# Gate and up projections of six blocks as seven block products instead of eight, with the order of work planned anew

## The chip, the cores and the metric

The kernel runs on one core of one Trainium2 chip. The number compared is the time of one execution on the device in microseconds (us), median of several runs. Engines: TensorE (PE; PEld is its weight load), VectorE (DVE), ScalarE (ACT), GpSimd (POOL), SyncE (SP, which here only starts DMAs).

## What is computed

The input x has 2 sequences of 4096 tokens with 256 features. Three branches are added:

```python
xn = layernorm(x)
h = tanh(xn @ W1.T + b1); s = h @ w2.T + b2          # a score per token
e = exp(s - max(s)); ctx = cumsum(e * xn) / cumsum(e)  # running mean over the sequence
attn = tanh(concat(ctx, xn) @ Wc.T + bc)
gate = xn @ (w_gate / 127).T; up = xn @ (w_up / 127).T   # integer weights, 768 hidden units
ffn = (silu(gate) * up) @ (w_down / 127).T
out = x + attn + ffn
```

The change touches `gate` and `up`.

## The kernel before, in words

The 8192 tokens are 16 blocks of 512. All of a block's matmuls are float16 with operands split into a high and a low part: x (times 1024) is `xt16[:, s, k, tokens]`, s = 0 high, s = 1 low, k one of the two halves of the 256 features. Integer weights are exact in float16 and need one part. For each block i the work is made of named steps:

- `Lp` or `Ln`, `Xh`, `Xm`, `Tx`: normalise, high part, low part, transposing DMAs into `xt16`.
- `Ss`, `S`, `Th`, `Sv`: scores (bias put into the bank by ACT, 12 matmuls of 256 columns, tanh, weighted sum). After the last block of a sequence the small softmax steps `V0`, `M1`, `Ex`, `M2` and so on.
- `Gg` and `Gu` (function `hidden`, matmul at L809): gate and up of hidden tile j (0 to 5, 128 units each), each 4 matmuls of 512 columns (two k, two parts of x) into one PSUM bank.
- `Sg` (ACT, L970): silu of the gate's bank to SBUF. `H` (DVE, L1204): times up, written back into up's bank. `Hh` (ACT, L977): high part of that to SBUF. `Hl` (DVE, L1209): low part.
- `D` (L777), two steps of 24 matmuls of 256 columns; its sum is added to x by `Da` (DVE, L1213).
- `N` (POOL, L1316 and L1321), `Sc` (DVE scan, L1227), `Ch` (ACT, L991), `Cl` (POOL, L1349): running mean. `Cs` (ACT, L915), `C` (L829 and L777, two steps of 24 matmuls of 256 columns), `Ct` (ACT, L984), `Ca` (DVE, L1218): the attention output. `Er`, `Ro`, `O` are DMAs.

The order on every engine is fixed when the program is built. `due_times` gives every step a due time, `STEP` a cost, and the class `Plan` hands out steps by due time as soon as it takes their needs (`needs`) to be met; it also chooses which of the 8 PSUM banks a group of matmuls gets, and so on whom it waits. Each engine then runs its list strictly in order, with semaphores between engines. `SEED_AHEAD` says how early ACT may put a bias into a bank; `SLACK` is time the plan leaves between a step and its user on another engine (TensorE 1.0 us, ACT and DVE 0.3 us).

## Time and profile before

| | us |
|---|---|
| median of 3 runs | 393.57 |
| the three runs | 391.73, 393.60, 393.57 |
| span of the profiled execution (first to last instruction) | 390.1 |
| PE busy | 384.7 |
| DVE, ACT, POOL busy | 290.2, 234.3, 213.2 |

The page gives the profiled execution by its span; its time on the clock of the runs isn't recorded, so what lies around the span is between 1.6 and 3.5 us, by the lowest and the highest run. In 40 slices of the span PE's busy digit is 9 in all but the first and the last; the granted clock is at its full level throughout.

### The profile page before, as it was taken

How to read it: one execution, taken by the hardware profiler on the slowest of the kernel's cores; microseconds unless marked ns; L12 is line 12 of the kernel's file. 1: busy time of each engine (PE TensorE's matmuls, PEld its weight loads, DVE VectorE, ACT ScalarE, POOL GpSimd, SP SyncE). 2: the span in 40 equal slices, each digit the busy share in tenths (PEclk: the TensorE clock that was granted, in tenths of full speed). 3: DMA queues.
4: the chain of work that ended last, by engine and by line, in shares of the span. 5: the costliest groups of instructions: out<-in, count | busy, mean ns of one | idle time of the engine just before them, and what ended most of it. 6: DMA issues, size and time to landing. Idle time of an engine off the chain costs nothing.

```text
span 390.1 us, 7869 instructions
## 1 busy us (share of the span) xinstructions
PE 384.7 (99%) x2735; PEld 268.3 (69%) x2735; DVE 290.2 (74%) x604; ACT 234.3 (60%) x436; POOL 213.2 (55%) x301
## 2 busy tenths in 40 slices
PE   8999999999999999999999999999999999999996
PEld 4557586666666686766877777768677676776765
DVE  6799999879697896966679965876776766754351
ACT  4785667498975659786466575463563644536260
POOL 1658797775529999895244415765455654502000
PEclk9999999999999999999999999999999999999999
DMA  8965356556644233676300014042131340100001
GB/s 257 332 220 86 84 106 175 93 150 92 170 96 98 54 99 66 134 145 101 81 29 29 28 41 154 27 150 79 43 94 46 80 106 4 54 29 28 29 27 62
DMA packets 55776, 36.82 MB, mean 94 GB/s; under 512 B 31922, under 2 KB 51635, under 8 KB 55731
## 3 DMA queue, kind: packets, MB, share of 16 engines
q1 hardware_dynamic: 55440, 35.99, 36.8%
q8 instruction: 24, 0.39, 0.4%
q10 hardware_dynamic: 290, 0.26, 0.2%
q14 instruction: 22, 0.17, 0.2%
HBM read 20.45 MB, written 8.45 MB: 74 GB/s over the span
## 4 chain that ended last, share of the span: by engine, by line
PE 99%; DVE 0%; issue 0%
PE bank L777 44%; PE bank L809 42%; PE bank L829 9%; PE bank L1474 1%; PE bank L756 1%; PE bank L748 0%; PE bank L741 0%; PE bank L1481 0%; DVE sg L1501 0%; PE bank L884 0%; PE bank L890 0%; DVE xres L1213 0%; PE bank L883 0%; PE bank L877 0%; PE bank L872 0%
## 5 line engine op out<-in xcount | busy, mean ns | idle before, releaser
L809 PE MATMUL bank<-xt,narrow 128*128 128x512 f16 x768 | 177.6, 379 | 0.0
L809 PEld LDWEIGHTS bank<-xt,narrow 128*128 128x128 f16 x768 | 75.2, 98 | 75.0
L777 PE MATMUL bank<-narrow,wide 128*128 128x256 f16 x792 | 96.4, 273 | 0.0
L777 PE MATMUL bank<-narrow,xt 128*128 128x256 f16 x744 | 90.2, 273 | 0.0
L1349 POOL TENSOR_TENSOR wide<-ex,wide 128x512 f16<-128x512 f32 x32 | 40.3, 1277 | 86.9 <-ACT wide L991 86.9
L970 ACT ACTIVATE sg<-bank 128x512 f32<-128x512 f32 x96 | 56.9, 595 | 49.9 <-PE bank L809 47.6
L777 PEld LDWEIGHTS bank<-narrow,xt 128*128 128x128 f16 x744 | 72.8, 98 | 18.0
L1204 DVE SCALAR_TENSOR_TENSOR bank<-bank,sg 128x512 f32<-128x512 f32 x96 | 66.1, 693 | 24.5 <-PE bank L809 22.2
L777 PEld LDWEIGHTS bank<-narrow,wide 128*128 128x128 f16 x792 | 77.5, 98 | 9.4
L977 ACT ACTIVATE wide<-bank 128x512 f16<-128x512 f32 x90 | 53.2, 594 | 46.8 <-DVE bank L1204 42.5
L1209 DVE TENSOR_TENSOR wide<-bank,wide 128x512 f16<-128x512 f32 x90 | 60.3, 677 | 9.7 <-ACT wide L977 8.5
L1227 DVE TENSOR_TENSOR_SCAN ex<-rows,ex 128x512 f32<-128x512 f32 x32 | 56.0, 1749 | 1.6 <-POOL ex L1321 1.6
L1321 POOL TENSOR_TENSOR ex<-ex,rows 128x512 f32<-128x512 f32 x32 | 43.6, 1364 | 8.9 <-DMA rows<-scratch 6.5
L1316 POOL TENSOR_TENSOR ex<-xt 128x512 f32<-128x512 f16 x32 | 46.4, 1449 | 0.2
L1213 DVE TENSOR_TENSOR xres<-bank,xres 128x512 f32<-128x512 f32 (+1 forms) x33 | 22.0, 667 | 29.9 <-PE bank L777 29.8
L829 PE MATMUL bank<-narrow,wide 128*128 128x256 f16 x312 | 38.3, 273 | 0.0
L984 ACT ACTIVATE bank<-bank 128x512 f32<-128x512 f32 (+1 forms) x33 | 18.8, 570 | 30.7 <-PE bank L777 30.7
L915 ACT ACTIVATE bank<-every 128x512 f32<-128x512 f32 (+1 forms) x63 | 37.1, 595 | 0.2 <-issue 0.2
L829 PEld LDWEIGHTS bank<-narrow,wide 128*128 128x128 f16 x312 | 30.5, 98 | 7.0
L1218 DVE TENSOR_TENSOR xres<-bank,xres 128x512 f32<-128x512 f32 x28 | 19.3, 688 | 17.8 <-ACT bank L984 17.7
L1189 DVE CUSTOM_DVE_ANT_0 bank<-bank,every 128x256 f32<-128x256 f32 x64 | 25.5, 443 | 4.8 <-ACT bank L964 4.8
L964 ACT ACTIVATE bank<-bank 128x512 f32<-128x512 f32 x32 | 18.7, 585 | 7.4 <-PE bank L777 7.4
(109 smaller groups left out, 259.0 us busy)
## 6 DMA issues: line engine op xcount, KB each, us to landing
rows<-scratch SPq DMA_DIRECT2D x16, 512.0 KB, 5.3
out_y<-xres SPq DMA_DIRECT2D x31, 256.0 KB, 2.1
xres<-in_x SPq DMA_DIRECT2D x15, 512.0 KB, 5.0
xt<-xt SPq DMA_TRANSPOSE x56, 2.5
wide<-in_wg SPq DMA_DIRECT2D x2, 384.0 KB, 5.3
wide<-in_wu SPq DMA_DIRECT2D x2, 384.0 KB, 6.6
wide<-in_wd SPq DMA_DIRECT2D x1, 768.0 KB, 8.7
wide<-in_wc SPq DMA_DIRECT2D x1, 512.0 KB, 10.4
```

Of the source, the lines that this page charges most:

```text
L777: return pe.matmul(dst, lhs, rhs, start=False, stop=stop, skip_group_check=True)
L809: mm = pe.matmul(b[:, :], pg.up(which, k, j), pg.xn(sx, k, tok), start=n == 0, stop=n == len(todo) - 1)
L829: mm = pe.matmul(dst, lhs, rhs, start=n == 0, stop=n == len(todo) - 1)
L915: act.activation(b[:, 0:n * D].rearrange("p (t d) -> p t d", t=n), row.to_broadcast([P, n, D]), ACT.Copy, scale=pg.sum_up).then_inc(done, 1)
L970: act.activation(sg[:, m % SG_RING, :], bank_of(pg, "Gg", i, n)[:, :], ACT.Silu, scale=pg.silu_scale).then_inc(a_sg, 1)
L977: act.activation(pg.h(0, m, slice(0, BLK)), bank_of(pg, "Gu", i, n)[:, :], ACT.Copy).then_inc(a_h, 1)
L1204: dve.scalar_tensor_tensor(out=dst, in0=b[:, :], scalar=pg.up_scale, in1=sg[:, m % SG_RING, :], op0=ALU.mult, op1=ALU.mult).then_inc(v_h, 1)
L1209: dve.tensor_tensor(pg.h(1, m, slice(0, BLK)), bank_of(pg, "Gu", i, n)[:, :], pg.h(0, m, slice(0, BLK)), ALU.subtract).then_inc(v_hlo, 1)
L1227: dve.tensor_tensor_scan(t, rows[:, i % 2, 1, :], t, 0.0 if first else ex[:, (i - 1) % EX_RING, n, BLK - 1:BLK], ALU.mult, ALU.add).then_i ...
L1316: pool.tensor_tensor(dst, xt16[:, 0, k, tok], xt16[:, 1, k, tok], ALU.add).then_inc(g_x, 1)
L1321: pool.tensor_tensor(dst, src, rows[:, i % 2, 0, :], ALU.mult).then_inc(g_ex, 1)
L1349: pool.tensor_tensor(pg.ctx(1, i, k, slice(0, BLK)), ex[:, i % EX_RING, k, :], pg.ctx(0, i, k, slice(0, BLK)), ALU.subtract).then_inc(g_cl ...
```

## The change

For blocks 9 to 14 (`FAST`) the steps `Gg` and `Gu` are gone. A pair of hidden tiles (a group q, 0 to 2) is computed with tokens in two halves A and B of 256, features in two halves k = 0, 1, and gate and up together: that is a 2 x 2 by 2 x 2 product of blocks, usually 8 block products, here 7 (`Qa` to `Qg`), each 4 matmuls of 256 columns (two hidden tiles, two parts of x). It needs four sums of weights (`Ks`, `sums16`, once) and, for each of these blocks, four sums of x (`Nt` on ACT normalises once more, `Tf` on POOL forms the sums, `Uh` on ACT and `Um` on POOL split them, `Ux` on SP transposes them by DMA into `forms`).

The seven products share partial sums. `Zs` (ACT) copies Qa's bank to a second one; `Qd` goes onto the first (gate of A), `Qc` onto the second; `Zv` (ACT) copies that to SBUF; `Qe` goes on top; `Yv` (ACT) copies Qb's bank to SBUF; `Wa` (DVE) adds it to Qe's bank into SBUF (up of B); `Qf` then goes onto that bank (up of A); `Qg` goes onto Qb's bank and `Ya` (DVE) adds Zv's copy (gate of B). `H` and `Hh` follow as before, but the product H is written to SBUF (`up_of`); the low part of the second of each pair moves from DVE to POOL (`Hp`). Storage comes from regions of `xres` and `xt` whose blocks are done, so `O` of blocks 0 to 4 gets semaphores of its own (`s_home`).

Besides, `SEED_AHEAD` goes from 2.5 to 9.05, the due times of `C` and `D` are tables, and `CHAIN` = 0.3 takes the place of TensorE's slack of 1.0 for the new steps: the whole order is planned anew.

```diff
-SEED_AHEAD = 2.5
+SEED_AHEAD = 9.05
+CHAIN = 0.3
+    "Qa": (TE, 0.44, 0.68), "Qb": (TE, 0.44, 0.68), "Qc": (TE, 0.44, 0.68), ...
+    "Wa": (VE, 0.62, 0.75), "Ya": (VE, 0.62, 0.75), "Ks": (VE, 3.8, 3.9), "Hp": (PO, 1.3, 1.4),
+FAST = tuple(range(9, 15))
+GROUPS = KH // 2
-        ctx = 38.0 + 3.7 * i if i < LAST else NBLK * KH
-        place += [(ctx + pr, ("C", i, pr)) for pr in shares(i)]
+        place += [(C_AT[i] + C_STEP * pr, ("C", i, pr)) for pr in shares(i)]
...
+            def product(kind, i, q):
+                first, second = slice(0, PAIR), slice(PAIR, BLK)
+                gate = ("Gg", i, 2 * q + (kind in ("Qb", "Qg")))
+                b = bank_of(pg, *gate) if kind in ("Qa", "Qb", "Qd", "Qg") else bank_of(pg, "Gu", i, 2 * q)
...
+                elif kind == "Qc":
+                    pe.wait_ge(a_zs, pg.nth("Zs", i, q))
...
+                    w, of_x, done = sums16[:, 1, :], lambda s: forms(i)[:, s, 1, second], p_qc
+                elif kind == "Qd":
+                    pe.wait_ge(a_zs, pg.nth("Zs", i, q))
+                elif kind == "Qe":
+                    pe.wait_ge(a_zv, pg.nth("Zv", i, q))
+                elif kind == "Qf":
+                    pe.wait_ge(v_wa, pg.nth("Wa", i, q))
+                else:
+                    pe.wait_ge(a_yv, pg.nth("Yv", i, q))
...
+                opens = kind in ("Qa", "Qb")
+                for e in range(2):
+                    j = 2 * q + e
+                    for s in range(2):
+                        mm = pe.matmul(b[:, e * PAIR:(e + 1) * PAIR], w[:, j * P:(j + 1) * P], of_x(s),
+                                       start=opens and (e, s) == (0, 0), stop=s == 1, skip_group_check=True)
+                mm.then_inc(done, 1)
...
+            elif kind == "Zs":
+                b = open_bank(act, pg, "Gu", i, 2 * n)
+                act.wait_ge(p_qa, pg.nth("Qa", i, n))
+                act.activation(b[:, :], bank_of(pg, "Gg", i, 2 * n)[:, :], ACT.Copy).then_inc(a_zs, 1)
+            elif kind == "Zv":
...
+                act.wait_ge(p_qc, pg.nth("Qc", i, n))
+                act.activation(later[group_number(i, n) % 2], bank_of(pg, "Gu", i, 2 * n)[:, :], ACT.Copy).then_inc(a_zv, 1)
...
+            elif kind == "Wa":
+                back, at = before_group(i, n, 2), group_number(i, n) % 2
+                if back:
+                    dve.wait_ge(g_hlo, pg.nth("Hp", back[0], 2 * back[1] + 1))
...
+                dve.wait_ge(a_yv, pg.nth("Yv", i, n))
+                dve.wait_ge(p_qe, pg.nth("Qe", i, n))
+                dve.tensor_tensor(second_up[at], half(bank_of(pg, "Gu", i, 2 * n)[:, :]), half(first_sum),
+                                  ALU.add).then_inc(v_wa, 1)
+            elif kind == "Ya":
+                b = bank_of(pg, "Gg", i, 2 * n + 1)
+                dve.wait_ge(a_zv, pg.nth("Zv", i, n))
+                dve.wait_ge(p_qg, pg.nth("Qg", i, n))
+                dve.tensor_tensor(b[:, :], b[:, :], later[group_number(i, n) % 2], ALU.add).then_inc(v_ya, 1)
...
+            elif kind == "Tf":
+                pool.wait_ge(a_nt, pg.nth("Nt", i, 1))
+                before = FORM_STEPS * (pg.nth("Tf", i, 0) - 1)
+                (a0, a1), (b0, b1) = ([xnat[:, pr, :, k * P:(k + 1) * P] for k in range(KD)] for pr in range(2))
+                pool.tensor_tensor(a0, b0, a0, ALU.subtract).then_inc(g_tf, 1)
...
+            elif kind == "Um":
+                pool.wait_ge(a_uh, pg.nth("Uh", i, k))
+                pool.tensor_tensor(xt16[:, k, :, D:BLK], xnat[:, k, :, :], xt16[:, k, :, 0:D],
+                                   ALU.subtract).then_inc(g_um, 1)
+            elif kind == "Hp":
+                m = KH * i + k
+                pool.wait_ge(a_h, pg.nth("Hh", i, k))
+                pool.tensor_tensor(half(pg.h(1, m, slice(0, BLK))), up_of(i, k),
+                                   half(pg.h(0, m, slice(0, BLK))), ALU.subtract).then_inc(g_hlo, 1)
```

What stands on TensorE around `D` of block 10. In the order of before L809 with `x4` is one `Gg` or `Gu`, L829 and L777 from `narrow,wide` are a `D` or the second half of a `C`, L777 from `narrow,xt` the first half of a `C`:

```order
L777 MATMUL bank5<-narrow,xt 128x256 x12
L777 MATMUL bank5<-narrow,wide 128x256 x12
L829 MATMUL bank6<-narrow,wide 128x256 x12
L777 MATMUL bank6<-narrow,wide 128x256 x12
L809 MATMUL bank7<-xt,narrow 128x512 x4
L829 MATMUL bank4<-narrow,wide 128x256 x12
L777 MATMUL bank4<-narrow,wide 128x256 x12
L809 MATMUL bank1<-xt,narrow 128x512 x4
L777 MATMUL bank2<-narrow,xt 128x256 x12
```

In the order of after, L1007 is one of the seven products: from `xt,narrow` it is Qa or Qd, from `xt,xres` Qg, from `xres,narrow` Qf, from `xres` alone Qb, Qc or Qe. L1031 and L933 are what L829 and L777 were:

```order
L1007 MATMUL bank4<-xres 128x256 x4
L1007 MATMUL bank7<-xres,narrow 128x256 x4
L1031 MATMUL bank5<-narrow,wide 128x256 x12
L933 MATMUL bank5<-narrow,wide 128x256 x12
L1007 MATMUL bank6<-xt,narrow 128x256 x4
L1031 MATMUL bank0<-narrow,wide 128x256 x12
L933 MATMUL bank0<-narrow,wide 128x256 x12
L1007 MATMUL bank4<-xres 128x256 x4
L1007 MATMUL bank3<-xt,xres 128x256 x4
L1007 MATMUL bank2<-xt,narrow 128x256 x4
L1007 MATMUL bank5<-xres 128x256 x4
L933 MATMUL bank1<-narrow,xt 128x256 x12
L933 MATMUL bank1<-narrow,wide 128x256 x12
```

`D` and `C` stand near where they stood, but the products between them wait for one another through other engines. The first row is Qc of block 11's second group, into bank4. After Qf of the group before, `D`, Qd and `D` comes Qe into the same bank4, which waits for `Zv`; after Qg, Qa, Qb and half of `C` comes Qf into bank4, which waits for `Wa`.

What stands on VectorE at the same place, before. L1204 is `H`, L1209 `Hl`, L1218 `Ca`, L1227 `Sc`, L1213 `Da`:

```order
L1209 TENSOR_TENSOR wide<-bank3,wide 128x512
L1209 TENSOR_TENSOR wide<-bank0,wide 128x512
L1218 TENSOR_TENSOR xres<-bank5,xres 128x512
L1227 SCALAR_TENSOR_TENSOR ex<-rows,ex 128x512
L1213 TENSOR_TENSOR xres<-bank6,xres 128x512
L1213 TENSOR_TENSOR xres<-bank4,xres 128x512
L1204 SCALAR_TENSOR_TENSOR bank1<-bank1,sg 128x512
L1209 TENSOR_TENSOR wide<-bank1,wide 128x512
```

And after. L1459 is `H` (written to `xt`; from `xt,sg` for the second of a pair), L1490 `Hl`, L1499 `Ca`, L1508 `Sc`, L1494 `Da`, L1469 `Wa`, L1475 `Ya`:

```order
L1459 SCALAR_TENSOR_TENSOR xt<-bank7,sg 128x2x256
L1499 TENSOR_TENSOR xres<-bank2,xres 128x512
L1459 SCALAR_TENSOR_TENSOR xt<-xt,sg 128x2x256
L1494 TENSOR_TENSOR xres<-bank5,xres 128x512
L1490 TENSOR_TENSOR wide<-xt,wide 128x512
L1508 SCALAR_TENSOR_TENSOR ex<-rows,ex 128x512
L1494 TENSOR_TENSOR xres<-bank0,xres 128x512
L1469 TENSOR_TENSOR xt<-bank4,xres 128x2x256
L1475 TENSOR_TENSOR bank3<-bank3,xres 128x512
L1459 SCALAR_TENSOR_TENSOR xt<-bank4,sg 128x2x256
L1459 SCALAR_TENSOR_TENSOR xt<-xt,sg 128x2x256
```

`Wa`, for which TensorE's next Qf waits, stands behind `H`, `Da`, `Hl`, `Sc` and `Da` in VectorE's list. `H` of the second of a pair and `Hl` now read two operands from SBUF, where before one of them came from PSUM.

## Rows read from the trace of the kernel before

**Rows 1.** The page: busy time by engine, then PE and its clock in 40 slices

```profile
PE 384.7 (99%) x2735; PEld 268.3 (69%) x2735; DVE 290.2 (74%) x604; ACT 234.3 (60%) x436; POOL 213.2 (55%) x301
...
PE   8999999999999999999999999999999999999996
...
PEclk9999999999999999999999999999999999999999
```

**Rows 2.** The page: the chain that ended last, by engine

```profile
PE 99%; DVE 0%; issue 0%
```

**Rows 3.** Waits of PE, whole span: engine line waited for: us, times, longest

```profile
PE bank L1474 <- DVE sg L1501: 1.6, 1, 1.6
```

**Rows 4.** The chain in order of time: start us, us, what

```profile
276.76 5.18 PE bank L809 x24
...
375.78 10.49 PE bank L777 x96
```

**Rows 5.** Groups of instructions: line engine op names shapes count | busy us, mean ns | idle before

```profile
L777 PEld LDWEIGHTS bank<-narrow,wide 128*128 128x128 f16 x792 | 77.5, 98 | 9.4
```

**Rows 6.** Busy time in the stretch of blocks 9 to 14: window, length, then each engine

```profile
213.35:354.90 141.55, 141.55 (x1019) 99.55 (x1018) 98.84 (x141) 73.62 (x133) 68.93 (x54) 1.00 0.22 66
```

**Rows 7.** Groups of DVE in that stretch: the scan

```profile
L1227 DVE TENSOR_TENSOR_SCAN ex<-rows,ex 128x512 f32<-128x512 f32 x19 | 30.9, 1628 | 0.0
```

**Rows 8.** Single lines: duration ns min/median/max, first and last start

```profile
L1227 DVE TENSOR_TENSOR_SCAN ex<-rows,ex x32: 1267/1756/2318, 122.6 to 341.4; 128x512 f32<-128x512 f32 x32
...
L1209 DVE TENSOR_TENSOR wide<-bank,wide x90: 656/680/693, 31.5 to 377.3; 128x512 f16<-128x512 f32 x90
...
L1349 POOL TENSOR_TENSOR wide<-ex,wide x32: 1148/1157/2084, 126.6 to 354.8; 128x512 f16<-128x512 f32 x32
...
L1316 POOL TENSOR_TENSOR ex<-xt x32: 1138/1155/2084, 118.3 to 337.6; 128x512 f32<-128x512 f16 x32
...
L1321 POOL TENSOR_TENSOR ex<-ex,rows x32: 1262/1270/2081, 119.5 to 339.7; 128x512 f32<-128x512 f32 x32
```

**Rows 9.** Timeline near 136 us, DVE and then POOL: start us, us, instruction

```profile
136.29 2.18 DVE L1227 TENSOR_TENSOR_SCAN ex<-rows,ex 128x512 f32<-128x512 f32 x1
138.40 0.66 DVE L1209 TENSOR_TENSOR wide<-bank,wide 128x512 f16<-128x512 f32 x1
138.98 0.67 DVE L1213 TENSOR_TENSOR xres<-bank,xres 128x512 f32<-128x512 f32 x1
...
136.24 1.16 POOL L1349 TENSOR_TENSOR wide<-ex,wide 128x512 f16<-128x512 f32 x1
137.35 2.07 POOL L1316 TENSOR_TENSOR ex<-xt 128x512 f32<-128x512 f16 x1
```

**Rows 10.** Timeline, 359 to 362 us: from one engine to the next

```profile
359.39 0.70 DVE L1204 SCALAR_TENSOR_TENSOR bank<-bank,sg 128x512 f32<-128x512 f32 x1 [2.23 <-PE bank L809]
360.19 0.60 ACT L977 ACTIVATE wide<-bank 128x512 f16<-128x512 f32 x1 [1.07 <-DVE bank L1204]
...
361.74 1.89 PE L809 MATMUL bank<-xt,narrow 128*128 128x512 f16 x8
361.94 0.58 ACT L984 ACTIVATE bank<-bank 128x512 f32<-128x512 f32 x1 [1.16 <-PE bank L777]
```

**Rows 11.** Timeline of ACT near 87 us: three instructions that wait for nobody

```profile
86.54 0.60 ACT L970 ACTIVATE sg<-bank 128x512 f32<-128x512 f32 x1
87.02 0.62 ACT L915 ACTIVATE bank<-every 128x512 f32<-128x512 f32 x1
87.54 0.64 ACT L947 ACTIVATE xt<-xt 128x512 f16<-128x512 f32 x1
```

**Rows 12.** Groups: VectorE on float16 with both inputs in SBUF

```profile
L1261 DVE TENSOR_TENSOR xt<-xt 128x768 f16<-128x768 f16 x1 | 1.5, 1504 | 0.0
...
L1258 DVE TENSOR_TENSOR xt<-xt 128x768 f16<-128x768 f16 x1 | 0.9, 918 | 0.0
```

More of the change, by code:

```diff
@@ L87 @@
 POOLED = tuple(range(1, 9))
+FAST = tuple(range(9, 15))
+GROUPS = KH // 2
+LOW_POOL = (1,)
+HOME = tuple(range(5))
 FIRST_T = 2
@@ L177, in due_times @@
         due[st] = now
-        now += STEP[st[0]][1]
+        now += STEP[st[0]][1] if st[0] not in ("Gg", "Gu") or st[1] not in FAST else 0.0
         end[st] = now
@@ L341, in needs @@
     if kind == "D":
-        return [(("Hl", i, k), 0.2 * k) for k in range(KH)] + ([(("Ct", i, x), 0)] if seeded(i, x) else []) \
+        low = [((low_of(half_of(x)), i, 2 * q + half_of(x)), 0.4 * q) for q in range(GROUPS)] if seven else \
+            [(("Hl", i, k), 0.2 * k) for k in range(KH)]
+        return low + ([(("Ct", i, x), 0)] if seeded(i, x) else []) \
             + [(("D", i, x - 1) if x else ("Wdh", 0, 0), 0)]
@@ L486, in start @@
         group = closed_by(st)
+        if st[1] in FAST and not self.wide and st[0] in ("H", "Hl"):
+            group = ("Gu", *st[1:]) if st[0] == "H" and st[2] % 2 == 0 else None
         if group is not None:
@@ L1193, in vector_step @@
                 m = KH * i + n
-                b = bank_of(pg, "Gu", i, n)
+                second = pg.fast(i) and n % 2
+                b = None if second else bank_of(pg, "Gu", i, n)
                 if pg.wide:
```

268 lines of the change are left out of this document (243 added, 25 removed).

## The prediction

> **What bounds the kernel now.** I read the page first: PE is busy for 384.7 of 390.1 us, its busy digit is 9 in every slice but the ends, and its clock is at the full level (2.4 GHz) throughout [rows 1]. A busy PE need not be PE at its peak, so the chain comes next: 99% of it is PE [rows 2]. Then the waits: PE waits once, 1.6 us at the start, and for nobody after that [rows 3]. So the time is the number of matmuls times their spacing, and every other engine is hidden. The spacing comes from the chain in order of time, where a stretch goes from the start of one group to the start of the next: 24 matmuls of 512 columns in 5.18 us are 215.8 ns each, 96 of 256 columns in 10.49 us are 109.3 ns each [rows 4]. (The mean durations of PE in the groups are longer, because matmuls overlap; they are of no use for a sum.)
>
> **What the change removes and adds on PE.** A block's gate and up are 12 steps of 4 matmuls of 512 columns: 48 x 0.2158 = 10.36 us. After, they are 3 groups of 7 products of 4 matmuls of 256 columns: 84 x 0.1093 = 9.18 us. Six blocks: 62.15 us go, 55.09 us come, 7.1 us saved. An eighth is 7.8 us; the rest is lost because two matmuls of 256 columns take 218.6 ns and one of 512 takes 215.8. Everything else on PE (the scores, `D`, `C`, softmax, block 15) keeps its count and shape. The weight loads rise from 48 to 84 a block, but one takes 98 ns [rows 5] and fits into the 109.3 ns of its matmul, as it does for all matmuls of 256 columns now.
>
> The Trainium skill has a rule that speaks against this ("TensorE: Matmul & The Clock Gate", Back-to-back issue gap): in a stream of weight load and matmul pairs it gives about 131 ns a matmul at 512 columns and 81 at 128. By it 36 more matmuls a block would cost more than their columns save. The spacings of this trace are far from these figures and close to columns over 2.4 GHz, so I give it no weight of its own beyond the rival below.
>
> **What it adds elsewhere, in the stretch of blocks 9 to 14.** That stretch is 141.6 us of unbroken PE now, with DVE 98.8, ACT 73.6 and POOL 68.9 busy [rows 6]. It should become 134.5 us.
> - ACT: 54 copies (`Zs`, `Zv`, `Yv`) at 0.49 us, the spacing of ACT when it waits for nobody (86.54, 87.02) [rows 11], 26.5 us; `Nt` and `Uh` of about four blocks, 8 steps at twice 0.49 and 9 at 0.52 (87.02, 87.54), 12.5 us. Together 112.6 of 134.5, 84%. It holds.
> - POOL: 17 `Hp` and 9 `Um` at 1.16 (L1349's median), 30.2 us; four `Tf` of 4 instructions of half of L1321's size, at (1.27 / 2) + 0.08 = 0.72, 11.5 us [rows 8]. Together 110.6, 82%.
> - DVE: 36 `Wa` and `Ya` come, 18 `Hl` go to POOL, at a spacing of 0.6 (138.40 to 138.98) [rows 9]: 10.8 us net. Together 109.6, 82%, if each instruction keeps its length.
> - `Ks`, four float16 additions, falls into block 7; the two nearest rows give 0.9 and 1.5 us each [rows 12], so 3.7 to 6 us in a stretch where DVE has more than that free. Nothing on PE. The 24 new transposing DMAs are issued from SP blocks ahead of their use, which hides them; I cost them at nothing.
>
> Outside the stretch the order changes too, but PE's steps are the same, and no engine gets more work except the first forms in blocks 6 to 8. I cost that at nothing; what hides it is the same distance between steps that hides everything now.
>
> **The term that is not a count: stalls.** DVE's instructions won't keep their length. The scan `Sc` takes 1267 ns at the least and 1756 in the median; POOL's three large ones 1150 to 1270 in the median and 2084 at the most [rows 8]. The timeline shows why: the scan that starts at 136.29 finds POOL's instruction of 136.24 at work, and ends 1.3 us after that one has ended; POOL's next one, of 137.35, takes 2.07 and ends 0.95 us after the scan [rows 9]. They take turns. `Hl` at L1209, with one operand in PSUM, never exceeds 693 ns in 90 instances [rows 8], so it is the scan's two SBUF operands that count. After the change 18 `H` and 18 `Hl` read two operands from SBUF as well. With POOL at work 0.8 of the time and a mean rest of 0.58 us, each waits 0.46 us on average: 16.6 us more on DVE, and the 19 scans, now stretched by 1628 - 1267 = 361 ns in this stretch [rows 7, 8], gain some 0.1 each. DVE comes to about 128 of 134.5 us, 95%. (The Trainium skill, "SBUF — State Buffer", Who interferes with whom, has this as a rule: a DVE instruction with two SBUF inputs contends with a GpSimd instruction that reads SBUF, and the loser blocks for the whole of the other. The trace agrees, 2.07 against 1.15 us, and the sum is the same by either.)
>
> What this costs PE hangs on cover. A bank goes from PE to ACT 0.20 us after the next matmul group starts (361.74, 361.94), a copy takes 0.58 to 0.60, and the next engine follows within 0.1 [rows 10]; so `Zs` or `Zv` needs about 0.85 us between two products and `Wa` (0.70 on DVE) 0.95. In the new order the nearest pairs are 4 products apart, 1.75 us: cover of 0.9 us for `Zv` five times, 0.8 for `Wa` once, the others 1.2 and more; one bank that goes from the first half of a `D` to the second has 0.4. Some 20 handovers in all have less than 1.5 us of cover, where before there were 3, and these were no stall. What lies before them in DVE's list is on average at hand, but `Wa` in the order shown stands behind `H`, `Da`, `Hl`, `Sc` and `Da`, two of them stretched by up to 1.2 us. And a late `Ya` or `H` holds up ACT, whose `Sg` and `Hh` wait for them ahead of the next `Zv`. The bounds: below, 0, because today 6.9 us of stretched scans in this stretch (19 x 0.361) [rows 7] pass nothing to PE; above, all 16.6. I take 2.3 us, one part in seven, nearer to the row that shows nothing passed.
>
> **Sum.** 390.1 - 7.1 + 2.3 = 385.3 us of span. Between span and median lie 3.5 us now, so 388.8 us by the median of 393.57. The lowest of the three runs lies 1.8 us below the median, and the low end of the range has to allow for a part of that.
>
> **Rivals.**
> 1. DVE's stretched instructions pass a third and more. For it: DVE at 95%, in-order lists, and a `Sc` of 2 us can stand ahead of any `Wa`. Against: PE's own stalls give DVE time to catch up, and most pairs have 2 to 4 us. At 0.36 of 16.6, 6 us: 390.1 - 7.1 + 6 + 3.5 = 392.5.
> 2. Slower: DVE becomes the bound of the stretch. The place is blocks 10 to 13, the price is (109.6 + 36 w) - 134.5, with w the mean wait of an `H` or `Hl` from SBUF. It decides from w = 0.69 us; from w = 0.89 the gain is gone, and at w = 1.0, nearly a whole POOL instruction each time, the stretch is 145.6 us, 11.1 more than it should be: 393.57 - 7.1 + 11.1 = 397.6. For it: POOL's instructions are twice as long as these, and each that had to wait starts at once when DVE frees the path, so DVE may find it taken again and again. Against: my estimate from the scans' stretch is half of it.
> 3. The matmuls of 256 columns don't keep 109.3 ns when weights come from `xres` and change with each. The change is worth nothing from 62.15 / 504 = 123 ns on. Every matmul of 256 columns in this trace already changes its weights, so I give it little: about 394.
> 4. No stall at all: 386.5.
>
> **Chances.** The forecast with stalls of 0 to 4.8 us (386.5 to 391.3, rival 4 among it) 0.60; rival 1 0.24; rival 2 0.13; rival 3 0.03. A measurement can tell 0.5%, 2.0 us, from no change: faster is below 391.6, slower above 395.5. Faster: 0.60 and a third of rival 1, 0.68. Same: the rest of rival 1 and rival 3, 0.18. Slower: rival 2, rounded up, 0.14. The forecast's own range is 386 to 391.3. For 8 in 10 the range has to reach over rival 1 to the border of rival 2: 385.8 to 394.6, which leaves out rival 2 and a few hundredths below.
>
> **What would show it.** In the profile after: the new line of the products with 504 matmuls of 256 columns and L809's successor with 480 of 512; in the chain the same 109.3 and 215.8 ns; PE busy some 377.5 us (384.7 - 7.1); waits of PE for ACT's copies and DVE's additions in the window from 213 to 350 us, in pieces below 1 us that sum to about 2.3. `H` from `xt` and `Hl` with a median above 0.9 us and a maximum near 1.8, while `Wa`, `Ya` and the `H` from a bank stay at 0.69. DVE above 90% busy there. The forecast is wrong if PE's waits sum to more than 5 us, if the clock falls, if PE waits outside blocks 9 to 14, or if the spacing of the new products is above 112 ns.

## The result: slower by 0.6%, and the profile after

The median of 20 runs went from 392.54 us to 394.88 us; the ratio is 1.006, with a 95% interval of 1.0043 to 1.0076. The prediction said 388.8 us; 394.88 lies 0.3 us above its range for 8 in 10 (385.8 to 394.6). What it called slower began at 395.5 us (chance 0.14), so by its own borders this is "same" (0.18), though the interval says that the kernel is slower. The profiled run took 394.6 us with a span of 392.8, so 1.8 us lie around the span, not the 3.5 that the prediction took from the difference to the median of three runs. In 8 of the 20 runs, those of 395.7 us and more, the mean granted clock of TensorE is 0.995 or 0.996; in the other 12 it is 0.998 or more.

The page of after: the busy rows (busy us, share of the span, instructions), then POOL's busy tenths in 40 slices and the granted clock. They answer to [rows 1].

```profile
PE 381.5 (97%) x2951; PEld 289.5 (74%) x2951; DVE 324.9 (83%) x626; ACT 278.4 (71%) x526; POOL 284.2 (72%) x355
...
POOL 1638797875537889898736968999999999983100
PEclk9999999999999999999999999999999999999999
```

POOL is at 9 tenths in every slice from the 26th to the 35th. The clock is at its full level as far as the trace records it: its records begin at 5.98 us in before and at 9.90 us in after, and what lies ahead of the first record is printed as full. So "throughout", as it was said of before, is not shown for the first 6 us. The same stretch as [rows 6], after (us, then busy us and instruction count of PE, PEld, DVE, ACT, POOL):

```profile
213.35:354.90 141.55, 136.41 (x1236) 119.72 (x1234) 127.20 (x156) 109.74 (x206) 132.49 (x97) 1.00 0.34 86
```

PE was busy for all of this window before; now it misses 5.1 us. DVE is at 90% and POOL at 94%. [Rows 3] had one wait, at the start. The waits of PE after (us in total, times, longest):

```profile
PE bank L1031 <- DVE wide L1490: 2.1, 2, 1.4
PE bank L1789 <- DVE sg L1816: 1.6, 1, 1.6
PE bank L1007 <- DVE xt L1469: 1.2, 2, 0.8
PE bank L1031 <- DVE xres L1499: 1.0, 1, 1.0
PE bank L897 <- DVE score L1432: 0.7, 1, 0.7
PE bank L1007 <- DVE xres L1494: 0.3, 1, 0.3
PE bank L1081 <- DVE flag L1552: 0.2, 1, 0.2
```

The second row is the old wait. The fifth is new and lies outside the stretch, at 17 us. All others wait for DVE: the down product for the low part of `H` (L1490) and for the bank that `Ca` (L1499) frees, a product for `Wa` (L1469) and for the bank that `Da` (L1494) frees, a small softmax step for L1552.

DVE's three kinds of instruction without an operand in PSUM, and POOL's `Hp`, in the same stretch (busy us, mean ns, idle time before them):

```profile
L1508 DVE TENSOR_TENSOR_SCAN ex<-rows,ex 128x512 f32<-128x512 f32 x19 | 36.2, 1903 | 4.1 <-POOL ex L1602 4.1
L1459 DVE SCALAR_TENSOR_TENSOR xt<-xt,sg 128x512 f32<-128x512 f32 x16 | 20.0, 1247 | 0.0
L1490 DVE TENSOR_TENSOR wide<-xt,wide 128x512 f16<-128x512 f32 x16 | 19.4, 1212 | 0.4 <-ACT wide L1185 0.4
...
L1636 POOL TENSOR_TENSOR wide<-xt,wide 128x512 f16<-128x512 f32 x16 | 23.9, 1495 | 1.6 <-ACT wide L1185 1.6
```

**Where the time went.** A measure that doesn't hang on modelled ends is the time from the start of one matmul to the start of the next, less its norm (109.2 ns for 256 columns, 215.8 for 512, and 56 for the few of 128). In all of the stretch of before this excess is 0.0 us. After it is 7.0 us, in 11 places between 220 and 349 us, of which the largest are 1.54, 1.21, 0.92 and 0.87. Five of the 11 end with `Wa` (2.3 us together), two with `Hl` (2.4), one each with `Ca` (1.21), `Da` (0.47) and L1552 (0.34), and one with ScalarE's copy `Zv` (0.24). In the first 20 us the excess is 3.75 before and 6.39 after. So: -7.1 (products) + 7.0 (stalls in the stretch) + 2.6 (start) = +2.5 us; the spans differ by 2.7.

**Two of the stalls, read.** The largest, from 345.2 us (1.54 us), ends with `Hl`; that of 0.92 us, from 348.5 us, ends with `Wa`. This is the chain of waits before the second (start us, us, what); `Hl`, which ended the first, stands in it too:

```profile
341.43 0.87 issue
342.30 0.66 DVE xt L1459
342.96 0.61 DVE bank L1475
343.57 0.66 DVE xt L1459
344.23 0.49 issue
344.73 0.05 DVEq L1468
344.78 0.37 issue
345.15 1.64 DVE wide L1490
346.79 2.10 DVE ex L1508
348.88 0.59 DVE xt L1469
```

DVE works without a gap and stands on the path. Its timeline (start us, us) and POOL's, at the same time:

```profile
343.48 1.74 DVE L1459 SCALAR_TENSOR_TENSOR xt<-xt,sg 128x512 f32<-128x512 f32 x1
345.15 1.64 DVE L1490 TENSOR_TENSOR wide<-xt,wide 128x512 f16<-128x512 f32 x1
346.71 2.17 DVE L1508 TENSOR_TENSOR_SCAN ex<-rows,ex 128x512 f32<-128x512 f32 x1
348.80 0.66 DVE L1469 TENSOR_TENSOR xt<-bank,xres 128x512 f32<-128x512 f32 x1
```

```profile
343.41 1.27 POOL L1602 TENSOR_TENSOR ex<-ex,rows 128x512 f32<-128x512 f32 x1
344.63 1.60 POOL L1650 TENSOR_TENSOR wide<-ex,wide 128x512 f16<-128x512 f32 x1
346.20 1.60 POOL L1636 TENSOR_TENSOR wide<-xt,wide 128x512 f16<-128x512 f32 x1
347.76 2.07 POOL L1597 TENSOR_TENSOR ex<-xt 128x512 f32<-128x512 f16 x1
```

Three DVE instructions in a row without an operand in PSUM take 5.6 us in place of 2.6 (0.68 twice, and the scan's 1.27 of [rows 8]). Each ends about 0.6 us (the scan 1.1) after one of POOL's has ended: they take turns. The down product waits for the second of them, and `Wa` (L1469), for which PE's product `Qf` waits, stands behind the third; it keeps its 0.66.

**The start.** Under ScalarE's rows of before at 11 us, and of after (start us, us; in brackets the idle time and what ended it):

```profile
11.70 0.30 ACT L920 ACTIVATE rstd<-mv,eps 128x4 f32<-128x4 f32 x1 [2.85 <-DVE mv L1040]
```

```profile
13.94 0.60 ACT L1119 ACTIVATE bank<-every 128x512 f32<-128x512 f32 x1 [3.38 <-DMA every<-in_biases]
14.48 0.28 ACT L1124 ACTIVATE rstd<-mv,eps 128x4 f32<-128x4 f32 x1
```

Before, the square root of block 1 (`Rq`) ran as soon as DVE had its statistics. In the new order the seed `Ss` of block 1's scores (L1119), which copies the broadcast biases, stands ahead of it in ScalarE's list, and their DMA lands only at 13.9 us. Everything behind the root is 2.8 us later: the normalised rows on POOL, and, behind it on ScalarE, the tanh of block 0's scores; DVE's last step on these scores (L1432) frees the bank that PE's transposes (L897) wait for.

The 2.6 us of the start are two things. From 12 to 20 us the excess is 0.43 us in before and 1.37 in after; these 0.94 us are that wait. Up to 12 us it is 3.32 and 5.02, and there PE waits for nobody new: its matmuls stand twice as far apart for longer. Those of 512 columns are 427 ns apart up to 5 us in before and up to 8 us in after, and 216 later. These are the spacings of the clock's two levels (e4 below has 213 ns for 256 columns at a granted clock of 0.50 and 109 at 1.00), and the trace's first clock record, at the full level, is at 5.98 us in before and at 9.90 in after. This rise comes early in eight of the 16 profiled runs and late in eight, with the seed in either place (last section), so it isn't counted against the change. e3, whose list begins like that of after and whose clock rises early (5.96 us), shows alone what the late root costs: PE waits 2.1 us, until 17.8 us. Where the clock rises late, PE comes to that place later and part of the wait is covered.

### The profile page after: what moved, and what is told of

Read it like the earlier page. It is cut to its first block and busy times, and to the rows that moved or that the text cites. A ratio compares the mean times of both kernels' runs of the same rounds, so it can differ in the third digit from the quotient of the medians.

```text
span 392.8 us, 8689 instructions
## 1 busy us (share of the span) xinstructions
PE 381.5 (97%) x2951; PEld 289.5 (74%) x2951; DVE 324.9 (83%) x626; ACT 278.4 (71%) x526; POOL 284.2 (72%) x355
## 5 line engine op out<-in xcount | busy, mean ns | idle before, releaser
L965 PE MATMUL bank<-xt,narrow 128*128 128x512 f16 x480 | 110.8, 379 | 0.0
L933 PE MATMUL bank<-narrow,wide 128*128 128x256 f16 x792 | 96.4, 273 | 0.0
L933 PE MATMUL bank<-narrow,xt 128*128 128x256 f16 x744 | 90.0, 273 | 0.0
L933 PEld LDWEIGHTS bank<-narrow,wide 128*128 128x128 f16 x792 | 77.5, 98 | 9.4
L933 PEld LDWEIGHTS bank<-narrow,xt 128*128 128x128 f16 x744 | 72.8, 98 | 13.9
L965 PEld LDWEIGHTS bank<-xt,narrow 128*128 128x128 f16 x480 | 47.0, 98 | 47.2 <-DVE xres L1494 0.2
L1508 DVE TENSOR_TENSOR_SCAN ex<-rows,ex 128x512 f32<-128x512 f32 x32 | 57.8, 1805 | 5.2 <-POOL ex L1602 5.2
L1650 POOL TENSOR_TENSOR wide<-ex,wide 128x512 f16<-128x512 f32 x32 | 46.3, 1452 | 13.9 <-ACT wide L1234 13.9
L1459 DVE SCALAR_TENSOR_TENSOR bank<-bank,sg 128x512 f32<-128x512 f32 x60 | 41.5, 696 | 10.2 <-PE bank L965 9.2
L1602 POOL TENSOR_TENSOR ex<-ex,rows 128x512 f32<-128x512 f32 x32 | 47.0, 1469 | 3.8 <-DMA rows<-scratch 1.4
L1119 ACT ACTIVATE bank<-every 128x512 f32<-128x512 f32 (+1 forms) x63 | 37.2, 593 | 7.2 <-DMA every<-in_biases 3.4
L1031 PE MATMUL bank<-narrow,wide 128*128 128x256 f16 x312 | 38.7, 273 | 3.1 <-DVE wide L1490 2.1
L1185 ACT ACTIVATE wide<-bank 128x512 f16<-128x512 f32 x54 | 31.6, 593 | 13.6 <-DVE bank L1459 11.7
L1490 DVE TENSOR_TENSOR wide<-bank,wide 128x512 f16<-128x512 f32 x54 | 36.1, 678 | 3.5 <-ACT wide L1185 2.9
L1494 DVE TENSOR_TENSOR xres<-bank,xres 128x512 f32<-128x512 f32 (+1 forms) x33 | 21.9, 665 | 19.5 <-PE bank L933 19.2
L1031 PEld LDWEIGHTS bank<-narrow,wide 128*128 128x128 f16 x312 | 30.3, 98 | 9.2 <-DVE wide L1490 2.6
L1636 POOL TENSOR_TENSOR wide<-xt,wide 128x512 f16<-128x512 f32 x18 | 26.2, 1458 | 9.4 <-ACT wide L1185 9.4
L1007 PE MATMUL bank<-xres 128*128 128x256 f16 x216 | 30.8, 273 | 0.1
L1432 DVE CUSTOM_DVE_ANT_0 bank<-bank,every 128x256 f32<-128x256 f32 x64 | 25.6, 444 | 4.4 <-ACT bank L1168 4.3
L1185 ACT ACTIVATE wide<-xt 128x512 f16<-128x512 f32 x36 | 22.3, 630 | 9.0 <-DVE xt L1459 8.9
```

The lines of the kernel that those rows point to most:

```text
L933: return pe.matmul(dst, lhs, rhs, start=False, stop=stop, skip_group_check=True)
L965: mm = pe.matmul(b[:, :], pg.up(which, k, j), pg.xn(sx, k, tok), start=n == 0, stop=n == len(todo) - 1)
L1007: mm = pe.matmul(b[:, e * PAIR:(e + 1) * PAIR], w[:, j * P:(j + 1) * P], of_x(s), start=opens and (e, s) == (0, 0), stop=s == 1, skip_grou ...
L1031: mm = pe.matmul(dst, lhs, rhs, start=n == 0, stop=n == len(todo) - 1)
L1119: act.activation(b[:, 0:n * D].rearrange("p (t d) -> p t d", t=n), row.to_broadcast([P, n, D]), ACT.Copy, scale=pg.sum_up).then_inc(done, 1)
L1185: act.activation(half(pg.h(0, m, slice(0, BLK))), up, ACT.Copy).then_inc(a_h, 1)
```

## The experiments

Two theories for the stretch: **contention** (DVE's instructions without a PSUM operand and POOL take turns, so DVE is late) and **POOL's load** (POOL itself is late and others wait for it). A third is **the order**: handovers planned too tight, whatever the lengths. "Stretch" in the table is the excess of matmul spacing between 205 and 360 us, "start" that in the first 20 us, split at 12 us: the first part goes with the rise of the clock, the second has the wait behind the late root. Both are from the profiled run. The last column counts the runs whose mean granted clock is below 0.997; in before it is 0.998 or more in every run that has a record.

| kernel | median, us | ratio to before (95%) | start | stretch | clock below 0.997 |
|---|---|---|---|---|---|
| before | 392.54 | | 3.32 + 0.43 | 0.0 | |
| after | 394.88 | 1.006 (1.0043 to 1.0076) | 5.02 + 1.37 | 7.0 | 8 of 20 |
| e1 order alone | 395.14 | 1.0078 (1.0055 to 1.0102) | 5.41 + 0.43 | 0.0 | 1 of 6 |
| e2 few POOL elements | 388.41 | 0.9909 (0.9880 to 0.9938) | 5.37 + 0.93 | 1.1 | 1 of 6 |
| e3 `Hl` from its bank | 390.77 | 0.9967 (0.9945 to 0.9989) | 3.79 + 2.54 | 3.5 | 4 of 12 |
| e4 low parts all on DVE | 398.67 | 1.0164 (1.0134 to 1.0193) | 5.01 + 1.24 | 11.4 | 4 of 5 |
| e5 order alone, late seeds | 392.32 | 0.9994 (0.9975 to 1.0013) | 5.05 + 0.43 | 0.0 | 0 of 12 |
| e6 after, late seeds | 392.68 | 1.0009 (0.9990 to 1.0029) | 3.55 + 0.43 | 7.2 | 0 of 12 |
| e7 e3 + late seeds | 389.25 | 0.9926 (0.9898 to 0.9955) | 3.81 + 0.43 | 3.4 | 0 of 6 |
| e8 three blocks, late seeds | 393.32 | 1.0018 (0.9999 to 1.0037) | 5.09 + 0.43 | 3.8 | 4 of 12 |
| e9 e6, one operand | 386.80 | 0.9857 (0.9835 to 0.9879) | 5.06 + 0.43 | 1.7 | 0 of 8 |
| e10 e2 + late seeds | 387.34 | 0.9877 (0.9850 to 0.9904) | 3.54 + 0.43 | 1.0 | 1 of 6 |
| e11 e7, margin 0.0 | 387.64 | 0.9893 (0.9864 to 0.9922) | 3.35 + 0.43 | 2.3 | 0 of 6 |
| e12 e7, margin 0.5 | 392.65 | 1.0012 (0.9991 to 1.0032) | 3.47 + 0.43 | 6.7 | 0 of 12 |
| e13 e6, margin 0.0 | 394.67 | 1.0060 (1.0040 to 1.0079) | 5.13 + 0.43 | 8.3 | 0 of 6 |
| e14 both banks kept | 386.87 | 0.9874 (0.9851 to 0.9896) | 3.59 + 0.43 | 0.4 | 0 of 6 |

### The order alone (e1) and the place of one seed (e5, e6)

e1 is the kernel before with the change's tables:

```
-SEED_AHEAD = 2.5
+SEED_AHEAD = 9.05
...
-        ctx = 38.0 + 3.7 * i if i < LAST else NBLK * KH
-        place += [(ctx + pr, ("C", i, pr)) for pr in shares(i)]
+        place += [(C_AT[i] + C_STEP * pr, ("C", i, pr)) for pr in shares(i)]
```

> Eight block products in every block of gate and up, with the order tables of the kernel after (start of the scores of a round moved to 9.05, the new tables for the products of C); the whole output is computed. If the new order itself stalls TensorE (the order theory), this kernel carries most of the loss already: 395 us or more, with waits of TensorE of 5 us and over. If the stalls come from the load that the seven products bring (both load theories), nothing is loaded here that was not loaded before: 391 to 394 us, within 0.5% of the kernel before, and TensorE waits under 2 us.

Measured: 395.14 us, as slow as the order theory said, but with no stall in the stretch at all and no new entry among PE's waits. So neither side of the expectation holds whole: the order does cost 3.0 us, but not by stalls among the products. The seed and then the root stand late here too:

```profile
13.16 0.60 ACT L917 ACTIVATE bank<-every 128x512 f32<-128x512 f32 x1 [2.50 <-DMA every<-in_biases]
13.70 0.28 ACT L922 ACTIVATE rstd<-mv,eps 128x4 f32<-128x4 f32 x1
```

But PE doesn't wait for them in this profiled run. Its excess from 12 to 20 us is the 0.43 of before; what it has more is all ahead of 12 us, where the clock rises late (first record at 10.85 us). So this profile shows none of the 3.0 us as a wait, and whose they are has to come from an edit. e5 takes the place of the first seeds back in e1, e6 in after:

```
+FIRST_SEEDS = (("Ss", 1), ("Ss", 2))
-            ... self.ahead(st) > SEED_AHEAD):
+            ... self.ahead(st) > (2.5 if st[:2] in FIRST_SEEDS else SEED_AHEAD)):
```

> Eight products everywhere and the new order tables (as the kernel with the order alone, 395.1 us), but the seed of the scores of block 1 (ScalarE's Ss1.0, which reads the copy of the biases that lands at 13.2 us) stands behind the square root Rq1.0 again, as before: the two first rounds keep the old bound of 2.5 for the seeds. Head-of-queue theory: the 3.0 us that the new order costs come from this one place, and the time is 391.5 to 393.0 us. If they come from the rest of the order (scores of later rounds, products of C) or from the clock's later rise, 394.5 us or more.

> The kernel after (seven products in blocks 9 to 14), with the same one edit: seeds of blocks 1 and 2 not before their old place. Head-of-queue theory: 2 to 3 us of the 394.9 go, 391.8 to 393.0 us, and TensorE's wait of 0.9 us at 17 us goes; the stalls of some 6 to 7 us between 219 and 349 us stay. If the start is set by the clock alone: 394 to 395.5 us.

Measured: 392.32 and 392.68, both as the head-of-queue theory had it. The plan moves other steps with the seeds as well (15 pieces of TensorE's list), but from 20 to 205 us PE's excess is 0.6 us at most in any of these kernels. The root is back at 11.74 us in e6:

```profile
11.74 0.30 ACT L1125 ACTIVATE rstd<-mv,eps 128x4 f32<-128x4 f32 x1 [2.65 <-DVE mv L1284]
```

So the rest of the order costs nothing, and the place of the first seeds costs 2.8 us (395.14 to 392.32) and 2.2 us (394.88 to 392.68). The stalls of the stretch are the same in e6 (7.2) as in after (7.0): the two losses are independent. The wait that the early seed brings is 2.1 us in the profile with an early rise of the clock (e3), 0.5 to 0.9 in three with a late one (after, e2, e4) and nothing in e1, whose biases land at 13.2 us and not at 13.8 to 13.9 as in the other four. The lowest runs differ by 2.2 us (e1 and e5) and 1.9 us (after and e6), as a wait of 2.1 would have it. With a late rise the wait is shorter, so the medians should differ by less than they do (2.8 and 2.2 us); why they don't is shown in part only. The mean granted clock is below 0.997 in 18 of the 49 runs with the seed early (after, e1 to e4) and in 5 of the 86 with it late. In after the median of those 8 runs is 396.1 us and of the other 12 394.1. What TensorE did before its clock fell in them isn't on record, but for one of e4, the only one that was profiled.

### Contention or POOL's load (e2, e3, e4, e7, e9, e10)

e2 keeps the order and shrinks POOL's work from block 7 on:

```
+FEW = 16
+                    n = FEW if i >= 7 else BLK
-                    pool.tensor_tensor(dst, xt16[:, 0, k, tok], ...
+                    pool.tensor_tensor(dst[:, 0:n], xt16[:, 0, k, tok], ...
```

> The kernel after with its order and its seven products kept, but POOL's instructions of the low part of H (Hp), of the prepared sums (Tf, Um), of the first of the two subtractions of N and of the low part of C (these two from block 7 on) shrunk to 16 columns: most of that work is left out. TensorE has the same instructions. If DVE's instructions with two operands in SBUF are lengthened by POOL's (contention theory), or if POOL's load delays the others (load theory), the products of H fall from 1247 ns towards 1150 or less, DVE's waits for POOL go, TensorE's stalls of 7 us go to under 2, and the time is 387 to 389 us. If the new order is what stalls (order theory), DVE and TensorE are as before and the time stays at 393 to 395 us.

Measured: 388.41; the stalls go to 1.1 us, `H` from SBUF to a mean of 718 ns and `Hl` to 790. The order with seven products is not what stalls. Every engine's list stands in the order of after, so this order alone doesn't stall TensorE. It doesn't part the two load theories, since POOL's own lateness is gone too.

e3 takes the second SBUF operand from `Hl` of the even tiles; e7 is e3 with late seeds. The plan's rules for this bank change with it (not shown), and so does the order:

```
-                dst = ... else up_of(i, n) if pg.fast(i) else up
+                dst = ... else up_of(i, n) if second else up
-                up = up_of(i, n) if pg.fast(i) else half(bank_of(pg, "Gu", i, n)[:, :])
+                up = up_of(i, n) if pg.fast(i) and n % 2 else half(bank_of(pg, "Gu", i, n)[:, :])
```

> The even tile of each pair writes H in place in its PSUM bank, and the high and low parts are taken from there, so that DVE's subtraction Hl (18 of them in blocks 9 to 14) reads one operand from SBUF in place of two. Contention theory: Hl falls from 1247 ns to the 680 ns that its bank form has, 18 x 0.57 = 10 us of DVE time go; the two places where the down product waits for Hl (0.87 and 1.54 us) go or shrink, and the time is 391 to 393 us. Load theory (POOL's amount of work is the cause): POOL is as busy as before (95%), stalls stay at 6 us or more, 394 to 395 us. Against both stands that the bank is held longer; if that decides, products wait for banks and the time is above 395 us.

> Both edits: the even tile's H stays in its PSUM bank for its low part (390.8 us alone), and the seeds of blocks 1 and 2 wait. If the two losses are independent they add: 390.8 - 2.5 = 387.5 to 389 us, 0.8 to 1.2% under the kernel before. If the loss at the start only covers other waits, no better than 390 us.

Measured: 390.77 and 389.25, within 0.3 us of what contention and independent losses had given, 4.1 and 3.4 us less than the kernels that they edit, with POOL nearly as full as in after (128.4 us of the window in e7, 132.5 in after). e7's stalls are 3.4 us. The waits for `Hl` at 318 and 345 us are gone; the largest that is left (1.1 us) is for ScalarE's silu.

e4 moves 18 low parts from POOL to DVE (`LOW_POOL = ()` in place of `(1,)`):

> The low part of H of every odd tile goes back from POOL to DVE (18 instructions). POOL loses 18 x 1.5 = 27 us in the stretch of 137 us (95% to 75%), DVE gains 18 x 0.68 to 1.25 = 12 to 22 us on its 122.7 us. Load theory with POOL as the bound: POOL's delays go, 391 to 393 us. Contention theory: DVE has more instructions of the kind that is lengthened and stands at 134 us or more of 137, so it becomes the bound: 397 to 402 us, with TensorE waiting for DVE.

Measured: 398.67. The window, and the granted clock in 40 slices:

```profile
213.35:354.90 141.55, 134.60 (x1196) 117.55 (x1194) 133.57 (x167) 107.82 (x203) 114.40 (x82) 0.98 0.33 84
```

```profile
PEclk9999999999999999999999999989999899999999
```

POOL falls to 114.4 us in the window and DVE rises to 133.6 of 141.55. Of the 11.4 us in the table 6.1 are three waits of PE for `Wa` behind DVE's list (3.26 and 2.46 us the longest) and 1.5 two waits for ScalarE's copies. Some 3.2 us are no wait: from 262.45 to 265.87 us and from 313.65 to 317.07 us the granted clock is 0.50, its lower level, and the matmuls of 256 columns stand 213 ns apart. Either time PE had just resumed after one of the two longest waits. This is rival 2 of the prediction in kind, with the price of the clock on top. It rules POOL's load out as the bound: less work on POOL made it worse. The time falls inside the expectation of contention.

e9 leaves the second operand out while order and POOL's work stay:

```
+                if second:
+                    dve.tensor_scalar(out=dst, in0=up, scalar1=pg.up_scale, scalar2=0.25, ...)
...
+                if pg.fast(i):
+                    dve.tensor_scalar(out=half(pg.h(1, m, slice(0, BLK))), in0=up, ...)
```

> The order and all of POOL's work of the kernel after with late seeds (392.7 us) are kept. In blocks 9 to 14 DVE's 18 instructions for H of the odd tiles and 18 for Hl of the even tiles, which read two operands from SBUF, read one of them only (a product with constants in place of the product with the silu and of the subtraction: that part of the computation is left out). Contention theory: without the second SBUF operand they are not lengthened (700 ns or less in place of 1247), DVE gains 36 x 0.55 = 20 us, the six largest stalls of TensorE (5.9 of 6.9 us) go or shrink to under 2 us in all, and the time is 386 to 388.5 us with POOL's share of the stretch still above 85%. POOL-load theory: POOL is as full as before, stalls and time stay, 391 to 393 us.

Measured: 386.80, stalls 1.7 us. The window, and DVE's two changed lines in it (busy us, mean ns, then the idle time before them):

```profile
213.35:354.90 141.55, 140.52 (x1277) 124.30 (x1276) 122.54 (x162) 114.52 (x216) 126.52 (x99) 1.00 0.36 88
```

```profile
L1496 DVE TENSOR_SCALAR wide<-xt 128x512 f16<-128x512 f32 x17 | 15.9, 933 | 0.7 <-ACT wide L1186 0.4
L1461 DVE TENSOR_SCALAR xt<-xt 128x512 f32<-128x512 f32 x17 | 15.7, 923 | 0.8 <-ACT sg L1178 0.8
```

Time and stalls came as forecast, every engine's list stands in the order of e6, and POOL is still at 89%, so POOL's load is ruled out a second time. But 700 ns was wrong: these instructions, with one SBUF operand, take 414 and 420 ns when POOL rests and 1042 and 1105 in the mean when it works throughout. So they contend as well, and e9 shows what shorter instructions on DVE give, not that one operand fewer ends the contention; `H` and `Hl` from a bank show that (next table). Only 0.3 us less per instruction, 10 us on DVE, was enough to take 5.5 us of stalls. (The Trainium skill, "SBUF — State Buffer", Who interferes with whom, names `tensor_scalar` among the instructions that can run in a mode with two ports and then contend. The trace agrees.)

> Seven products, late seeds, and POOL's work shrunk as in the run with few POOL elements (388.4 us with early seeds): most of POOL's work from block 7 on is left out. If the loss at the start and the stalls in the stretch are all that ate the gain of 7.1 us, this gives 388.4 - 2.4 = 385 to 386.5 us, no more than 1.5 us above 392.3 - 7.1 = 385.2. If something else was lost (the start's gain hidden, spacing of the products), 387.5 us or more.

Measured: e10, 387.34, 0.8 us above the expectation and 0.2 below the other case. Its profiled run, one of the faster, has a span of 384.8, which is 390.1 - 7.1 + 1.0 (stalls) + 0.2 (start) and 0.6 more. Of these 0.4 are a wait of PE for DVE at 110 us, which all kernels with late seeds but e14 have. The gain of the products is there when nothing is in its way.

**Sorted by cover.** The trace shows the same in after. For DVE's instructions of one shape, the mean length when POOL was at work during none, and during at least 95%, of it:

| after | POOL idle | POOL at work |
|---|---|---|
| `H`, `xt<-xt,sg` | 686 ns (3) | 1517 ns (7), at most 1750 |
| `Hl`, `wide<-xt,wide` | 680 (2) | 1357 (11), at most 1690 |
| `H`, `bank<-bank,sg` | 693 (13) | 696 (24), at most 733 |
| `Hl`, `wide<-bank,wide` | 684 (13) | 676 (24), at most 693 |
| statistics of the layernorm, `stats<-xres` | 411 (15) | 410 (19), at most 421 |

The last row reads one operand, from SBUF, and isn't lengthened; `tensor_scalar` of e9 reads one from SBUF as well and is.

### How much the order adds (e8, e11, e12, e13), and both banks (e14)

e8 has seven products in blocks 9 to 11 only (`FAST = tuple(range(9, 12))`), with late seeds.

> Seven products in blocks 9 to 11 only, eight in 12 to 14, seeds of blocks 1 and 2 late. TensorE's work falls by 3 x 1.18 = 3.5 us against the kernel before. Load theories: the stalls belong to the blocks with seven products, 0.34 + 0.30 + 1.21 + 0.24 + 0.22 = 2.3 us up to block 11, so 392.1 - 3.5 + 2.3 = 390.5 to 391.5 us, and POOL's busy share of the later blocks falls. If the loss came from the order of work as such, it would be as large as with six blocks: 392.5 us or more.

Measured: 393.32, above the expectation; stalls of 3.8 us in three blocks, where after has 2.3 up to block 11 and e6 2.5. Two are of 1.56 and 1.35 us, and at 266 us DVE's timeline shows what PE's product waits for:

```profile
260.41 1.57 DVE L1491 TENSOR_TENSOR wide<-xt,wide 128x512 f16<-128x512 f32 x1
261.91 1.75 DVE L1460 SCALAR_TENSOR_TENSOR xt<-xt,sg 128x512 f32<-128x512 f32 x1
263.58 0.68 DVE L1500 TENSOR_TENSOR xres<-bank,xres 128x512 f32<-128x512 f32 x1
264.18 0.68 DVE L1476 TENSOR_TENSOR bank<-bank,xres 128x512 f32<-128x512 f32 x1
264.78 2.33 DVE L1509 TENSOR_TENSOR_SCAN ex<-rows,ex 128x512 f32<-128x512 f32 x1
267.02 0.66 DVE L1470 TENSOR_TENSOR xt<-bank,xres 128x512 f32<-128x512 f32 x1
```

It is the same chain, at another place: each variant gets its own order, and what a given length of queue costs depends on whether `Wa` happens to stand behind a scan. A dose per block can't be read from this.

e11 and e12 set the margin that the order keeps ahead of the seven products (`CHAIN`) to 0.0 and 0.5 in e7; e13 sets it to 0.0 in e6.

> The kernel with Hl from the bank and late seeds (389.25 us), with the margin that the order of work keeps ahead of each of the seven products set from 0.3 to 0.0 us. If the remaining stalls of 3.7 us come from handovers planned too tight, this makes them more: 390 us or more. If they come from places where the load is lengthened by more than any such margin, no change beyond 0.3%: 388.3 to 390.

> The same kernel with that margin set to 0.5 us. Tight-handover theory: fewer stalls, 387.5 to 389 us. If the margin only moves products behind other work and blocks banks for longer, the stalls move elsewhere: 389.5 to 393 us.

> The kernel after with late seeds (392.7 us) and the margin ahead of the seven products at 0.0 in place of 0.3 us; DVE keeps all its instructions without an operand in PSUM. If the margin alone gave the 1.6 us that it gave beside the bank edit (389.25 to 387.64), this is 391 us and the bank edit is worth 3.4 us at either margin. If the stalls are at the places where lengthened instructions feed TensorE and the margin was just a matter of where they fall, 391.5 to 393.5 us. If the tight order was the cause all along, 388 us or less.

Measured: e11 387.64, faster than either case of its expectation; e12 392.65, as the second case had it; e13 394.67, slower than all three of its cases. With DVE relieved the tighter margin gained 1.6 us; with DVE as in after it lost 2.0; the wider one lost 3.4. So handovers planned too tight aren't the cause. But the order has a share: e11 and e12 have the same load on DVE (117.3 and 117.1 us of the window) and stalls of 2.3 and 6.7 us. The bank edit, with the order that the plan makes of it, is worth 3.4 us at a margin of 0.3 and 7.0 at 0.0.

e14 is e7 and also leaves the silu of the odd tiles in its bank, so that `H` reads it there:

```
-SEED_AHEAD = 9.05
+SEED_AHEAD = 12.0
-CHAIN = 0.3
+CHAIN = -0.1
...
+                b = bank_of(pg, "Gg", i, n)[:, :]
-                act.activation(sg[:, m % SG_RING, :], bank_of(pg, "Gg", i, n)[:, :], ACT.Silu,
+                act.activation(b if pg.fast(i) and n % 2 else sg[:, m % SG_RING, :], b, ACT.Silu,
...
-                in1=half(sg[:, m % SG_RING, :])
+                in1=half(bank_of(pg, "Gg", i, n)[:, :] if second else sg[:, m % SG_RING, :])
```

> Both banks kept: H of the even tiles stays in its bank for Hl and the silu of the odd tiles stays in its bank for H, so that none of the 36 instructions is without an operand in PSUM; late seeds, margin of the seven products -0.1, bound of the seeds 12.0. Contention theory: DVE's 36 instructions take 0.69 us each, DVE is at 108 us of 135 and TensorE waits for none of them. The price is a bank held longer for each odd tile. If it is smaller than what is left of the stalls (2.5 us in the best kernel so far, 387.6 us), 385.5 to 387.5 us; if the banks decide, 388 to 391 us with products that wait for ScalarE's seeds or for free banks.

Measured: 386.87 us, as contention had it, the whole computation, 1.3% below the kernel before and 2.0% below after. Its window and the changed lines of DVE:

```profile
213.35:354.90 141.55, 140.19 (x1280) 124.67 (x1278) 107.12 (x154) 110.97 (x212) 122.20 (x99) 1.00 0.35 85
```

```profile
L1505 DVE TENSOR_TENSOR_SCAN ex<-rows,ex 128x512 f32<-128x512 f32 x19 | 29.5, 1552 | 0.6 <-POOL ex L1599 0.6
...
L1487 DVE TENSOR_TENSOR wide<-bank,wide 128x512 f16<-128x512 f32 x18 | 12.2, 679 | 1.3 <-ACT wide L1187 1.1
...
L1456 DVE SCALAR_TENSOR_TENSOR xt<-xt,bank 128x512 f32<-128x512 f32 x17 | 11.5, 677 | 0.1
```

`H` and `Hl` are at 677 and 679 ns, the scan at 1552 against 1903 in after, DVE at 107 us against 127, and POOL, with all its work, at 122 against 132: it had been lengthened as well. Stalls are 0.4 us. What e14's two other settings (margin and bound) give by themselves wasn't run.

## Why the prediction was wrong, point by point

- **Products, -7.1 us: right.** The new matmuls stand 109.3 ns apart, those of 512 columns 215.8 [rows 4]; rival 3 is out. The counts are those forecast (504 new, 288 fewer of 512 columns), and e10 and e14 show the gain in the time. PE's busy time fell by 3.2 us only (to 381.5, forecast 377.5): it counts the slow matmuls of the start as busy, and a part of each wait.
- **Order outside the stretch at nothing: failed.** This is the first wrong step, worth 2.2 to 2.8 us by the medians of e5 and e6. The reason given, the distance between steps, doesn't hold in the first 20 us, where an engine's list stands behind DMAs that land one after the other. The bound on the seeds let ScalarE take block 1's seed early, and no row was read for when its operand lands. A list of ScalarE's first ten steps beside the landing of the biases' copy would have shown it.
- **DVE lengthened by 0.46 us per instruction: right in kind, low in size.** `H` and `Hl` were 1247 and 1212 ns in the stretch (in the prediction's terms 0.56 more), and the scan 1903 where 1628 plus 0.1 were forecast: some 20 + 5 = 25 us, not 18. The cause of the miss is POOL: forecast at 110.6 us without its own waits for DVE and found at 132.5 of 141.55. POOL's `Hp` took 1495 ns in the mean where 1157 was taken from L1349 [rows 8]. (In [rows 9] the scan ends 1.07 us after POOL's instruction, not 1.3; the sum doesn't use it.) Each makes the other longer, and with POOL at 94% rather than 82% DVE nearly always finds it at work.
- **One seventh of it passed to PE, 2.3 us: failed, 7.0 passed.** This is the larger error, and it has two halves: 25 us were lengthened and not 16.6, and 0.28 of it passed and not 0.14. The share was taken near the zero of before, but that is the zero of a DVE at 70% of the stretch; after has 90%. The share isn't a matter of DVE's load alone (0.4 us of stalls at 76% in e14, 3.4 at 84% in e7, but 2.3 and 6.7 at 83% in e11 and e12), and how much of it is load and how much the place of `Wa` and `Hl` in the list stays open. The names were right: PE waits for `Wa`, `Hl` and for banks that DVE frees.
- **The clock:** the forecast left its fall and waits outside the stretch at nothing and named both as signs of being wrong. Both came: the wait at 17 us, and a mean granted clock of 0.995 or 0.996 in 8 of the 20 runs.
- **Around the span, 3.5 us:** 1.8 in fact. The median of three runs lay 1 us above that of twenty. That made the forecast 1.7 us too high and hid part of the error.
- **Together:** 390.1 - 7.1 + 7.0 + 2.6 = 392.6 of span, against 385.3 forecast; of the 2.6 us 0.9 are the seed's wait and 1.7 the later rise of the clock in the profiled run. Rival 1 had the stalls nearly to size (6 us). What made a kernel as fast as before (e6, 392.68) a slower one was not rival 2 but the start. e4 comes near to rival 2: DVE at 94%, 398.67 us where 397.6 was worked out, but this price holds some 3.2 us of the lower clock, which rival 2 didn't have, so the closeness is in part luck.

## What to carry to other kernels

When work is moved onto a vector engine that shares its path with another, lengthen both engines' instructions in the forecast. Count as free of this only what a trace shows free: here all instructions with an operand in PSUM, and the statistics with one operand in SBUF, but not `tensor_scalar` between two places in SBUF. Keeping two intermediates in their banks, with the order planned anew and two of the plan's settings changed, gave 5.8 us (e6 to e14), most of the 7.1 us of arithmetic that was saved. An instruction that stands earlier in an in-order list takes with it whatever its operand waits for: before a reordering is costed at nothing, read when that operand lands. And a stall share taken from a kernel whose vector engine has gaps can't be carried over to one where it has few.
